# The first batch's keys, queries and quantised weights in another order in a four-step transformer block

## What is computed

```python
x = x + xcond0(layernorm(x), ctx, ctx, tau, delta, ...)   # 16 heads, 375 context positions
x = x + ffn0(layernorm(x), w1, conv_w, conv_b, w2)        # weights to -1, 0, 1; activations to 8 bits
x = x + xcond1(ctx, layernorm(x), len, pt, W_a, W_c)      # window of 16 around pt, Gaussian weight
x = x + ffn1(layernorm(x), W1, b1, W2, b2, Wr, br)        # best of 8 experts for each row
```

## Time and profile before

| | |
|---|---|
| median of three runs | 406.36 us |
| profiled execution, own time | 408.17 us |
| its span | 406.30 us |
| mean granted clock of TensorE | 0.946 of full |
| busy: TensorE, VectorE, ScalarE, GpSimd | 85%, 60%, 49%, 46% |
| DMA traffic | 52.26 MB, 129 GB/s on average |

### The profile page before, as it was taken

One profiled execution on the slowest core, in us unless ns is written; L12 is line 12 of the kernel. 1 busy time (PEld: TensorE's weight loads), 2 busy tenths in 40 slices (PEclk: granted clock), 3 DMA queues, 4 the chain that ended last, 5 costly groups with the idle time before them and its releaser, 6 DMA issues.

```text
span 406.3 us, 8560 instructions
## 1 busy us (share of the span) xinstructions
PE 343.7 (85%) x2865; PEld 254.8 (63%) x2865; DVE 243.2 (60%) x579; ACT 201.0 (49%) x541; POOL 187.5 (46%) x236
## 2 busy tenths in 40 slices
PE   6517598798999897998989799887996999999993
PEld 2304475566866666766758566543553999999982
DVE  3266836478889687887876884787457532232220
ACT  2402666777786686776965657443010523323320
POOL 6312734388395594783961816631014124224222
PEclk9857879999999899999997989999998999999998
DMA  8963482644837548558277110898611111211211
GB/s 237 327 127 90 103 188 62 159 110 97 185 136 183 119 134 196 97 163 207 53 195 167 53 66 14 265 387 304 223 31 52 53 41 35 65 38 43 54 42 42
DMA packets 36696, 52.26 MB, mean 129 GB/s; under 512 B 10495, under 2 KB 28744, under 8 KB 36390
## 3 DMA queue, kind: packets, MB, share of 16 engines
q1 hardware_dynamic: 28716, 34.78, 33.3%
q10 hardware_dynamic: 6288, 12.33, 9.1%
q0 software_dynamic: 1648, 4.59, 3.9%
HBM read 42.81 MB, written 9.31 MB: 128 GB/s over the span
## 4 chain that ended last, share of the span: by engine, by line
PE 56%; DVE 14%; DMA 13%; SPq 8%; issue 4%; ACT 2%; POOL 2%; POOLq 0%; DVEq 0%; ACTq 0%
PE ps L596 54%; DMA W<-d_q 5%; DVE ps L1815 5%; SPq L513 3%; SPq L523 3%; PE ps L600 3%; DVE W L1932 2%; DMA d_delta<-W 2%; DMA d_q<-hold 2%; DMA W<-nmT 1%; SPq L494 1%; DMA W<-d_delta 1%; DMA proj<-in_WkT 1%; DVE W L1712 1%; DVE hold L1712 1%
## 5 line engine op out<-in xcount | busy, mean ns | idle before, releaser
L596 PE MATMUL ps<-W 125*32 125x112 f32 (+2 forms) x1280 | 93.3, 271 | 32.8 <-DMA W<-d_q 15.4
L596 PEld LDWEIGHTS ps<-W 125*32 125x32 f32 (+2 forms) x1280 | 63.6, 127 | 59.5 <-issue 24.4
L1815 DVE TENSOR_REDUCE ps<-ps 112x2 f32<-112x750 f32 x64 | 60.5, 945 | 35.9 <-PE ps L596 35.2
L1277 ACT ACTIVATE W<-ps 125x448 f32<-125x448 f32 x96 | 50.5, 548 | 25.2 <-PE ps L596 24.5
L596 PE MATMUL ps<-hold,proj 128*128 128x128 f32 (+2 forms) x288 | 50.6, 322 | 2.8 <-ACT W L1205 2.0
L1453 ACT ACTIVATE hold<-ps,consts 128x128 f32<-128x128 f32 x88 | 25.0, 369 | 49.5 <-PE ps L596 49.5
L1094 ACT ACTIVATE hold<-ps 128x224 f32<-128x224 f32 (+5 forms) x72 | 25.3, 354 | 41.4 <-PE ps L596 21.2
L596 PEld LDWEIGHTS ps<-hold,proj 128*128 128x128 f32 x288 | 38.1, 192 | 9.7 <-ACT W L1205 2.6
L596 PE MATMUL ps<-onesb 128*128 128x512 bf16 x160 | 43.0, 403 | 1.4 <-POOL hold L1472 1.4
L1692 POOL DMA_INDIRECT out_x<-hold x11 | 15.9, 1447 | 56.7 <-DVE hold L2183 56.7
L596 PE MATMUL ps<-W,hold 128*128 x176 | 40.9, 386 | 0.0
(11 more groups left out here) (176 smaller groups left out, 570.1 us busy)
## 6 DMA issues: line engine op xcount, KB each, us to landing
W<-in_L_ffn_W SPq DMA_DIRECT2D x10, 1024.0 KB, 12.6
W<-in_L_ffn_W ACTq DMA_DIRECT2D x6, 1024.0 KB, 5.3
d_k<-W SPq DMA_DIRECT2D x16, 281.2 KB, 3.3
W<-d_k SPq DMA_DIRECT2D x16, 281.2 KB
hold<-in_ctxT SPq DMA_DIRECT2D x8, 375.0 KB, 4.3
W<-d_k SPq DMA_DIRECT2D x16, 187.5 KB
W<-d_q SPq DMA_DIRECT2D x48, 56.0 KB, 3.3
d_x<-hold ACTq DMA_DIRECT2D x8, 224.0 KB, 4.0
```

Source lines behind the costliest of these rows:

```text
L596: return pe.matmul(o, lhsT=l, rhs=r, start=start, stop=stop, skip_group_check=True)
L1277: act.activation(pexp[g % 2][0:LT, t, :], pE[n % 2][0:LT, 0:HG * T], ACT.Exp).then_inc(exp_done, 1)
L1815: dve.tensor_reduce(mx[:, 2 * i:2 * i + 2], pS[0:T, :, 0:L], X, ALU.max).then_inc(mx_done, 1)
```

## The change

Four things are done, the first three for batch 0 alone.

1. SyncE loads w1T, w2T, WaT and WcT after the second keys' read; ScalarE did it at the start. The sums on VectorE come after batch 0's maxima, the product of the sums on TensorE at the head of the next iteration, and the rounding of w2T after batch 1's maxima. `w_cast` stays where it is.
2. The second half of the keys is made behind the queries, on TensorE and on ScalarE.
3. The rows are normalised on VectorE, straight from mean and power; a small activation at the start takes the table load.
4. In every batch the queries are read by halves of eight heads, three DMAs each, the copies of one part made by one broadcast read. Pair 0 waits for the first half, pair 4 for the second.

```diff
--- before.py
+++ after.py
@@ SyncE @@
                 if b >= 2:
-                    sp.wait_ge(qst_loaded[b % 2], 96 * (b // 2))
+                    sp.wait_ge(qst_loaded[b % 2], 48 * (b // 2))
+                    sp.wait_ge(qst_loaded[2 + b % 2], 48 * (b // 2))
...
-            def p_qread(b):
+            def p_qread(b, m):
...
-                src = d_q[b % 2].rearrange("m t (d h) l -> (t d) m (h l)", h=HM)
-                for r, (tq, _) in enumerate(TERMS):
-                    sp.dma_start(qst[b % 2][16 * r:16 * r + 16].rearrange("p (m h) l -> p m (h l)", m=DC),
-                                 src[16 * tq:16 * tq + 16]).then_inc(qst_loaded[b % 2], 16)
+                src = d_q[b % 2][m].rearrange("t (d h) l -> (t d) (h l)", h=HM)
+                dst = qst[b % 2][:, HM * m:HM * m + HM, :]
+                for t, (lo, n) in enumerate(((0, 3), (48, 2), (80, 1))):
+                    sp.dma_start(dst[lo:lo + 16 * n].rearrange("p h l -> p (h l)"),
+                                 src[16 * t:16 * t + 16].unsqueeze(0).to_broadcast([n, 16, HM * T])).then_inc(qst_loaded[2 * m + b % 2], 16)
...
+            @batch
+            def w_ffn(b):
+
+                if b == 0:
+                    for n, w in enumerate(("w1T", "w2T")):
+                        sp.dma_start(nat_f[n], A[w]).then_inc(f_loaded, 16)
+                    sp.dma_start(WaT[:, :, :], A["WaT"]).then_inc(wlate_loaded, 16)
+                    sp.dma_start(WcT[:, :, :], A["WcT"]).then_inc(wlate_loaded, 16)
...
-                p_qread(i - 1)
+                p_qread(i - 1, 0)
+                p_qread(i - 1, 1)
                 w_win(i - 1)
                 p_kwrite(i - 1, 1)
                 p_ctx(i)
                 p_kread(i - 1, 1)
+                w_ffn(i - 1)
@@ TensorE @@
-                pe.wait_ge(k_evac, 2 * b + 2)
+                pe.wait_ge(k_evac, 1 if b == 0 else 2 * b + 2)
                 pe.wait_ge(xn0_ready, b + 1)
...
-            def p_k(b, m):
-
+            def p_k(b, m, first):
+
+                if first != (b == 0 and m == 1):
+                    return
...
-                if m == 1:
+                if m == 1 and b == 0:
+                    pe.wait_ge(q_evac, 1)
+                if m == 1 and b >= 1:
                     pe.wait_ge(k_evac, 2 * b + 1)
...
                 if i == NP // 2:
                     pe.wait_ge(kst_loaded[2 + b % 2], 64 * (b // 2 + 1))
+                    pe.wait_ge(qst_loaded[2 + b % 2], 48 * (b // 2 + 1))
...
             for i in range(B + 6):
+                w_sum(i - 2)
                 t_xqT(i - 3)
                 a_scoresT(i - 2, 7)
                 a_scores(i - 1, 0)
...
                 p_q(i)
+                p_k(i, 1, True)
                 u_wc(i - 4)
                 t_onT(i - 2)
-                w_sum(i - 1)
                 a_max(i - 1)
@@ ScalarE @@
                     act.dma_start(WvT[:, :, :], A["WvT"]).then_inc(wv_loaded, 16)
-                    act.dma_start(WoT[:, :, :], A["WoT"]).then_inc(wlate_loaded, 16)
-                    act.dma_start(WaT[:, :, :], A["WaT"]).then_inc(wlate_loaded, 16)
-                    act.dma_start(WcT[:, :, :], A["WcT"]).then_inc(wlate_loaded, 16)
-
-            @batch
-            def w_ffn(b):
-
-                if b == 0:
-                    for i, n in enumerate(("w1T", "w2T")):
-                        act.dma_start(nat_f[i], A[n]).then_inc(f_loaded, 16)
+                    act.dma_start(WoT[:, :, :], A["WoT"]).then_inc(wo_loaded, 16)
+                    act.wait_ge(ones_made, 1)
+                    act.activation(qf[:, 0, 0:1], onesf[:, 0:1], ACT.Identity, bias=onesf[:, 1:2], scale=0.25)
...
                 p_qm(i - 22)
+                p_kf(i - 22, 1, True)
+                p_kh(i - 22, 1, True)
                 p_V2(i - 24)
@@ GpSimd @@
-                if b == END and which >= 2:
+                if (b == END and which >= 2) or (b == 0 and which == 0):
                     pool.tensor_tensor(rstd[:, which, s], ve[:, which:which + 1], expo[0:T, :], ALU.pow).then_inc(ln_rs[which], 1)
                     return
@@ VectorE @@
+            def p_ln(b):
+
+                if b == 0:
+                    dve.wait_ge(ln_rs[0], 1)
+                    ts(xn0[:, :], x0[0][:, :], mv[:, 0, 0:1], rstd[:, 0, 0:1], ALU.subtract, ALU.mult).then_inc(xn0_ready, 1)
...
                 w_quant(i - 3, 0)
                 t_xq(i - 4)
-                w_quant(i - 3, 1)
...
-                w_sum(i - 1)
                 a_max(i - 2, 2)
...
                 p_stats(i)
+                p_ln(i)
                 a_max(i - 2, 5)
...
                 a_nmT(i - 2)
+                w_quant(i - 3, 1)
+                w_sum(i - 2)
                 w_delta(i)
```

More of the change, by code:

```diff
@@ L348, in pixart_block @@
         qr_made = sem("qr_made")
-        qst_loaded = [sem(f"qst_loaded{i}") for i in range(2)]
+        qst_loaded = [sem(f"qst_loaded{i}") for i in range(4)]
         qt3_ready = sem("qt3_ready")
@@ L375, in pixart_block @@
         wlate_loaded = sem("wlate_loaded")
+        wo_loaded = sem("wo_loaded")
         wqv_loaded = sem("wqv_loaded")
@@ L681, in p_v @@
                     pe.wait_ge(cxT_loaded[b % 2], 16 * (b // 2 + 1))
-                if half == 0 and b <= 1:
-                    pe.wait_ge(q_evac, b + 1)
+                if half == 0 and b == 0:
+                    pe.wait_ge(k_evac, 2)
+                if half == 0 and b == 1:
+                    pe.wait_ge(q_evac, 2)
                 if half == 0 and b >= 2:
@@ L1155, in p_ln @@
             def p_ln(b):
[L1157 removed]
                 if b >= 1:
+                    act.wait_ge(ln_rs[0], b + 1)
                     act.wait_ge(xn0T_ps, b)
[L1160 to L1161 removed]
+                    act.activation(xn0[:, :], x0[b % 2][:, :], ACT.Identity, bias=nmr[:, 0, b % 2:b % 2 + 1],
+                                   scale=rstd[:, 0, b % 2:b % 2 + 1]).then_inc(xn0_ready, 1)
             @batch
@@ L1197, in p_kf @@
             @batch
-            def p_kf(b, m):
+            def p_kf(b, m, first):
+                if first != (b == 0 and m == 1):
+                    return
                 if b == 0:
@@ L1207, in p_kh @@
             @batch
-            def p_kh(b, m):
+            def p_kh(b, m, first):
+                if first != (b == 0 and m == 1):
+                    return
                 act.wait_ge(k_evac, DC * b + m + 1)
```

27 lines of the change are left out of this document (12 added, 15 removed).

## The result

The changed kernel takes **431.36 us** (median of 5 runs, 430.57 to 434.71) against 406.36 for the one before (5 runs beside them, 403.2 to 407.95). The ratio is 1.067, with a 95% interval of 1.063 to 1.071: slower by 25 us. The forecast was 404.6, its upper end 408.4. The profiled execution of the changed kernel took 434.71 us for a span of 433.0.

What follows compares the result with a forecast made beforehand. Bound by a loop of TensorE scores, VectorE maxima and DMA trips through HBM, not one full engine or bytes. Terms -8.0 + 2.0 + 5.9 + 1.3 + 0.5 - 3.5 = -1.8 took 406.36 to 404.6 us; range 401.4 to 408.4.

Steps and rivals of the forecast that it cites:

- The halves (-3.5): Score stages of batches 3 to 6: reading queries by halves shortens waits for d_q, -3.5 us, bounds 0 and 6.
- the 168.5: Batch 5: estimated landing, in us, of the last second-half key read, with the fifth pair starting at 169.34.
- Rival (b): Fifth pair, every batch: query waits become waits for the second half's keys; costs 3.5 us, total 408.1; chance 0.18.
- First scores (-8.0): Start of batch 0: first scores come 8.0 us sooner, at 20.4 instead of 28.26; bounds -7.5 and -8.8.
- The weights (+2.0, bounds 0 and 3.5): Batch 0's first transposed scores: d_ge, read behind SyncE's weight loads, delays them to 41.9 instead of 39.9; +2.0 us.
- The cover of 0.3 us: Batch 0: second-half keys land at about 28, their scores due at 28.3, so making them later costs nothing.
- The new wait (+5.9): Batch 0, before transposed scores 7: TensorE stops for sums' product, scale, quantisation, cast and exp 5; +5.9 us, bounds 5.3 and 6.3.
- The clock (+1.3, bounds 0 and 3.4): Batch 1's scores: low TensorE clock after the pause slows four pairs, +1.3 us.
- The second quantisation (+0.5): After batch 1's maxima: it runs beside GpSimd's query parts and slows them, +0.5 us, bounds 0 to 1.3.
- Rival (a): d_ge's small read passes the weights and lands in 3.4 us, so +2.0 falls away: total 402.6; chance 0.17.
- Rival (c): After the pause, TensorE stays at half clock another 3.4 us and sets the pace: +1.9 us, total 406.5; chance 0.15.

## Why the forecast was wrong

**The halves (-3.5) are the step that failed.** I took the six half reads for the same work as six whole ones: 1.3 us of issue for the first three, and the rest as before. They take 3.87 us instead of 2.65 (three plain key reads take 1.25), and the write behind them can be read back 1.2 to 1.5 us later. With both, the second keys come later, and the fifth pair waits for them: 12.9 us from batch 2 on (14.9 in all, less batch 0's 1.99), where it waited 0.76 in batch 2 before. The change's halves cost 13.9 us against whole reads, and 20 us alone: +13.5 in the loop for a term of -3.5 with bounds 0 and 6. Without the repetition my term was right in size: 413.5 against 417.5 in the changed kernel, and 403.0 against 407.2 before, 4.0 and 4.2 us for a forecast of 3.5. The first pair's waits for queries did go, as I had it; the form of the reads broke the rest. The slack of the second keys was a weak row of that term: no trace shows the landing of a key read, so the 168.5 was my estimate, and without the repetition the fifth pair still waited 0.43 to 2.92 us from batch 3 on.

The rule for it was there to be read. The Trainium skill, "DMA: Bandwidth & Descriptors", section "Rules for kernel authors", says that an outermost dimension of size c below 16, such as a leading broadcast of c copies, confines the whole DMA to at most c engines. By that rule 84 KB a half went through at most 3 engines and 56 KB through at most 2. The traces agree in effect: late landing and late second keys, and neither with the same six issues when nothing repeats. They don't show the engines that carried a read, so the number of engines is cited and not shown, and a read with a short outermost dimension that repeats nothing was not tried. Repetition as such is not slow: the read of d_ge repeats 128 times, 187.5 KB, takes 0.43 to issue and lands in 4.2 in the kernels before and after. Nor is every such read slow to issue: that of d_delta has three rows outermost, each eight times over (17.6 KB), and takes 0.30. So what makes the query reads' issue longer stays open.

```profile
W<-d_ge SPq DMA_DIRECT2D x8, 187.5 KB, 4.2
...
W<-d_q SPq DMA_DIRECT2D x16, 84.0 KB
```

**Rival (b)** named the place (the fifth pair's wait for the second keys) and was priced at 3.5 us with a chance of 0.18. Its price was bounded by what the halves could win, where it should have been bounded by what sits in front of the second keys' write.

**First scores (-8.0)**: measured 6.1 (22.13 for a forecast of 20.4). The query write went out at 14.24 for 13.7, and the first maximum comes at 22.22 without the repetition against 22.67 with it. So 0.5 of the 1.7 us lie ahead of the write and some 0.5 in the reads' form; the rest is landing that I took too short.

**The weights (+2.0, bounds 0 and 3.5)**: the first transposed scores were forecast at 41.9 and stand at 51.17, 9.3 us off, the second large miss. I followed d_ge, which landed at 40.04, 5.5 us later than forecast. In front of it stood the load of x for batch 2, which I left out: VectorE needs it between two maxima. That load set the time: batch 1's keys, which hang on d_ge, were written at 44.24, but the maxima were ready to be read only at 46.48. The cover of 0.3 us that I gave to the second keys was gone too: their pair stood at 32.39, not at 28.3. SyncE came to their write at 23.80, not at 20.4, because the query reads took 1.2 us longer and a small write ahead of it waited 1.8 us for ScalarE. In the version with whole reads, the loads moved behind x and d_ge brought batch 0's last maximum 4.5 us forward.

**The new wait (+5.9)**: right. From the first transposed scores to batch 1's first maximum it took 13.92 us instead of 8.04, +5.9, and the gap stood where I had it, with the cast inside. The gap itself is 5.41 us, so 0.5 of the 5.9 lie elsewhere in that stretch, and that the sizes agree to 0.1 us is in part luck.

**The clock (+1.3, bounds 0 and 3.4)**: batch 1's eight maxima took 14.4 us instead of 11.2, +3.2. I had priced four pairs; the clock was at 0.50 over all of 60 to 70 us and at 0.81 from 70 to 80, so all eight ran behind it at least in part.

**The second quantisation (+0.5)** can't be told from other shifts. **Rival (a)** fell with d_ge's landing at 40, 9.2 us after its issue. **Rival (c)**, the long low clock, came true in batch 1, with +3.2 in place of 1.3.

Laid end to end, the stretches are -6.1 for the first scores, +9.4 up to the transposed scores of batch 0 (from 22.13 to 51.17 it is 29.04, 19.66 before), +5.9, +3.2, and 13.5 for the loop: 25.9, by which the last maximum of batch 7 is later. They must add up to that, so the sum shows where the time went and not why; the whys rest on the runs above.

## What to carry to other kernels

Cutting a DMA into two is only free if each half is as good a DMA as the whole: look at a repeated outermost dimension with few copies, and at every write that is issued behind it. When a large load is moved on a queue, list all loads behind it and who needs each first, including those for batches two ahead that an engine reads in the middle of the present one. And where six small reads serve repeated data, see whether the other operand can be reordered so that neither repeats: that alone was worth 2% here.

## What the runs showed of the hardware

- The query reads that repeat 16 rows few times are slow to issue as well as to land. The first of a half (3 copies, 84 KB) took 0.78 us to issue and the second (2 copies) 0.67; the plain third 0.42, as the plain reads elsewhere. The 128-copy read of d_ge took 0.43, and that of d_delta, 17.6 KB with three rows eight times over, 0.30.

```profile
114.02 0.78 SPq L516 DMA_DIRECT2D W<-d_q  x1
```

```profile
114.84 0.67 SPq L516 DMA_DIRECT2D W<-d_q  x1
```

- Such reads delay what is issued behind them on the queue. In batches 3 and 4 it is 5.5 to 6.2 us from a key write to its read back, against 3.3 to 4.9 behind six or twelve plain reads. Behind the three whole reads (400.56), where the write goes out 1.4 us sooner after the first read, it is 4.8 and 5.9, so plain reads can delay a write as well. From the first query read to the read back it is 9.5 to 10.2 us with the repeating reads, 6.8 to 7.6 with six plain ones and 6.2 to 7.2 with three.
- Each further plain read costs some 0.4 us of SyncE's time at 28 to 168 KB: three whole reads took 1.26 us and landed in 4.1 to 4.2, six took 2.65 and landed in 3.3, six half reads 2.62. Twelve in a row took 5.41 and 6.78, 0.45 to 0.57 each.
